# Shared expert: unit 3's gate products ahead of unit 2's up products, and the lower part of the second token half on GpSimd

## The chip, the cores and the metric

One core of one Trainium2 chip. The metric is the device time of one execution in microseconds (us), as the median of several runs. Engines are called by their names in the profile: PE is TensorE (PEld its weight loads), DVE is VectorE, ACT is ScalarE, POOL is GpSimd, SP is SyncE, which only issues DMAs here.

## The reference

A mixture of experts with all eight routed experts taken and one shared expert, with a residual. B = 8 batches of S = 128 tokens, D = 128, F = 512, all float32:

```python
g = jnp.einsum('bsd,edf->ebsf', h, Wg)
u = jnp.einsum('bsd,edf->ebsf', h, Wu)
expert_outs = jnp.einsum('ebsf,efd->ebsd', jax.nn.silu(g) * u, Wd)
expert_output = jnp.einsum('be,ebsd->bsd', gating_probs, expert_outs)
shared = jnp.einsum('bsf,fd->bsd', jax.nn.silu(h @ Sg) * (h @ Su), Sd)
sg = shared_gate_prob[:, :, None]
return x + (1.0 - sg) * expert_output + sg * shared
```

## The kernel before

The 1024 tokens are two halves of 512 columns (`HALVES`), tokens along the free axis and the model width along the partitions. F is cut into four slices of 128. An expert is eight *units*: unit k is slice k % 4 of half k // 4. For a unit TensorE computes the gate product into a PSUM bank `g_ps`, the up product into `u_ps`, and, two units later (`LAG`), adds the unit's share of the down product to `y_ps`. ACT applies silu to `g_ps`; DVE multiplies with `u_ps` into `h_ps` (`hidden`, L408); ACT rounds that to `h_hi` (`hidden_hi`, L334); DVE subtracts to get `h_lo` (`hidden_lo`, L413). In this text gate(k), up(k), down(k), silu(k), hidden(k), h_hi(k) and h_lo(k) are these steps of unit k.

Precision: every float32 operand is split into an upper part in a rounded format (`_hi`) and the remainder (`_lo`), and each product is three matmuls, hi x hi, hi x lo and lo x hi. So each of gate, up and down is three matmuls of 128x512, nine a unit. The upper parts are copies (`first_hi`, `w_hi_slice`, `xs_hi_half`), the lower parts differences (`first_lo`, `slice_lo`, `half_lo` on POOL; `hidden_lo` on DVE).

Each engine runs its own program, written out by hand in order, and engines meet at semaphores: a `wait_ge` holds its engine, and what stands behind it, until the counter is there. There are two banks each of `g_ps`, `u_ps` and `h_ps`: gate(k) waits for silu(k-2), up(k) for hidden(k-2), hidden(k) for h_lo(k-2).

The shared expert comes first, with the weights in buffer 0. Its units 0 and 1 are written out apart (L515 to L540) while tokens and weights still arrive. Units 2 to 7 are the loop at L542: gate(k), up(k), down(k-2). Its first waits also cover the prepared operands:

```python
                pe.wait_ge(first_dve_hi, 2)
                pe.wait_ge(first_pool_lo, 4 if k == BANKS else 5)
```

`first_dve_hi` 2 is DVE's CAST of the shared down weights (`first_hi(DOWN, 0, 4)`, L436, executed at L385); `first_pool_lo` 4 and 5 are the first slice and the other three slices of their lower part on POOL (L234, L235, executed at L224), which wait for that CAST.

The second token half reaches the core as `x_blk`, is turned by DVE (L400) into `x_t[:, 1]`, rounded by ACT (`second_x_hi`, L316, semaphore `x_hi_done[2]`), and DVE takes the difference `x_lo[:, 1]` at L440. gate(4) is the first to use it.

DVE's order in this stage is: hidden(0), CAST of the down weights, hidden(1), h_lo(0), `x_lo` of the second half (L440), hidden(2), h_lo(1), `factors` (L424 and L428, the coefficients of experts and batches), hidden(3), h_lo(2), hidden(4), h_lo(3) and so on. POOL's is: the lower parts of the shared gate and up weights, those of the down weights, slice 0 of expert 0's weights (L244), then the scaled tokens (L239) once the factors are there. ACT's is, per unit: silu(k), one piece of preparation for the next expert (`split_next`: L324 or L320), h_hi(k).

SP's load of expert 1 into buffer 0 (L196) waits for `first_pool_lo` 5.

The eight routed experts follow (`routed_expert`), with the same unit and nine matmuls of 128x512 each; then the end: two output forms, by DVE's transpose and by TensorE.

Of the kernel before, what the change touches and what calls it, by code (L numbers as in the profile page):

```python
# [8 lines left out]
ALU = mybir.AluOpType  # L9
# [4 lines left out]
LAG = 2  # L14
BANKS = 2
# [9 lines left out]
def build(nc, x, gates, shared_gate, Wg, Wu, Wd, Sg, Su, Sd, out):  # L25
# [3 lines left out]
    NF = F // P  # L29
    UNITS = NF * HALVES  # L30
# [18 lines left out]
    with ctx:  # L49
        def sbuf(name, shape, dtype):  # L50
            return ctx.enter_context(nc.sbuf_tensor(name, shape, dtype))

        def sem(name):
            return ctx.enter_context(nc.semaphore(name))
# [5 lines left out]
        x_t = sbuf("x_t", [P, HALVES, N], FP32)  # L60
        x_hi = sbuf("x_hi", [P, HALVES, N], FP32R)
        x_lo = sbuf("x_lo", [P, HALVES, N], FP32R)
# [25 lines left out]
        def banks(name, n):  # L88
            return [ctx.enter_context(nc.psum_tensor(f"{name}{i}", [P, N], FP32)) for i in range(n)]

        y_ps = banks("y_ps", HALVES)
        g_ps = banks("g_ps", BANKS)
        u_ps = banks("u_ps", BANKS)
# [18 lines left out]
        x_hi_done = [sem(f"x_hi_done{i}") for i in range(3)]  # L112
        first_gate_hi = sem("first_gate_hi")
        x_lo_done = sem("x_lo_done")
        x_t_done = sem("x_t_done")
        x1_turned = sem("x1_turned")
        first_act_hi = sem("first_act_hi")
# [2 lines left out]
        first_pool_lo = sem("first_pool_lo")  # L120
# [31 lines left out]
        def f32(t):  # L152
            return t.bitcast(FP32)

        def tokens(t):

            return t.rearrange("p (q b r) -> p q b r", q=NQ, b=HBATCH)

        def by_batch(c):

            return c.unsqueeze(1).unsqueeze(3).to_broadcast([P, NQ, HBATCH, PER])
# [55 lines left out]
        def gpsimd_program(pool):  # L217
            pool.memset(ident[:, :], 0.0).then_inc(ident_zeroed, 1)
            pool.wait_ge(ident_zeroed, 1)
            pool.affine_select(out=ident[:, :], in_=ident[:, :], compare_op=ALU.not_equal, fill=1.0,  # L220
                               base=0, pattern=[[-1, P]], channel_multiplier=1).then_inc(ident_built, 1)

            def first_lo(k, n, m):
                pool.tensor_tensor(w_lo[0][:, k, n:m, :], w_raw[0][:, k, n:m, :],  # L224
                                   f32(w_hi[0][:, k, n:m, :]), ALU.subtract).then_inc(first_pool_lo, 1)

            pool.wait_ge(first_act_hi, 1)
            first_lo(GATE, 2, 4)
            pool.wait_ge(first_act_hi, 2)
            first_lo(UP, 0, 2)  # L230
            pool.wait_ge(first_dve_hi, 1)
            first_lo(UP, 2, 4)
            pool.wait_ge(first_dve_hi, 2)
            first_lo(DOWN, 0, 1)  # L234
            first_lo(DOWN, 1, 4)  # L235

            def scale(e, h):
                c = coef[:, e - 1, h * HBATCH:(h + 1) * HBATCH]
                pool.tensor_tensor(tokens(xs[:, h, :]), tokens(x_t[:, h, :]), by_batch(c), ALU.mult)\  # L239
                    .then_inc(xs_done, 1)  # L240

            def slice_lo(n, buf, slices_before):
                pool.wait_ge(w_hi_done, slices_before + n + 1)
                pool.tensor_tensor(w_lo[buf][:, :, n, :], w_raw[buf][:, :, n, :],  # L244
                                   f32(w_hi[buf][:, :, n, :]), ALU.subtract).then_inc(w_lo_done, 1)

            def half_lo(h, buf, halves_before):
                pool.wait_ge(xs_hi_done, halves_before + h + 1)
                pool.tensor_tensor(xs_lo[buf][:, h, :], xs[:, h, :], f32(xs_hi[buf][:, h, :]),  # L249
                                   ALU.subtract).then_inc(xs_lo_done, 1)  # L250

            def prepare(e, buf, halves_before, slices_before):
                for h in range(HALVES):

                    pool.wait_ge(xs_hi_done, halves_before - HALVES + h + 1)
                    pool.wait_ge(xs_lo_done, halves_before - HALVES + h + 1)
                    scale(e, h)
                for kind, n in PREPARE:
                    if kind == "slice":
                        slice_lo(n, buf, slices_before)  # L260
                    else:
                        half_lo(n, buf, halves_before)


            slice_lo(0, 1, 0)
            pool.wait_ge(coef_ready, 1)
            pool.wait_ge(x_t_done, 2)
            pool.wait_ge(x1_turned, 1)
            for h in range(HALVES):
                scale(1, h)  # L270
            slice_lo(1, 1, 0)
            half_lo(0, 1, 0)
            slice_lo(2, 1, 0)
            half_lo(1, 1, 0)
            slice_lo(3, 1, 0)
            with pool.Fori(0, E // 2 - 1) as i:
                for q in range(2):
                    prepare(2 * i + 2 + q, q, 2 * HALVES * i + HALVES * (q + 1),
                            2 * NF * i + NF * (q + 1))
            prepare(E, 0, HALVES * (E - 1), NF * (E - 1))  # L280

            for h in range(HALVES):
                pool.wait_ge(base_scaled, h + 1)
                pool.tensor_tensor(base_t[:, h, :], base_t[:, h, :], x_t[:, h, :], ALU.add)\
                    .then_inc(base_done, 1)
# [97 lines left out]
        def vector_program(dve):  # L383
# [27 lines left out]
            def hidden_lo(n, k):  # L411
                dve.wait_ge(h_hi_done, n + 1)
                dve.tensor_tensor(h_lo[k % HB][:, :], h_ps[k % BANKS][:, :], f32(h_hi[k % HB][:, :]),  # L413
                                  ALU.subtract).then_inc(h_lo_done, 1)
# [7 lines left out]
            def factors():  # L422
                dve.wait_ge(sg_loaded, DMA)
                dve.tensor_scalar(not_sg[:, :], coef[:, E, :], -1.0, 1.0, ALU.mult, ALU.add)\  # L424
                   .then_inc(one_minus, 1)
                dve.wait_ge(gates_loaded, DMA)
                dve.wait_ge(one_minus, 1)
                dve.tensor_tensor(coef[:, 0:E, :].rearrange("p e b -> p b e"), gates_sb[:, :, :],  # L428
                                  not_sg[:, :].unsqueeze(2).to_broadcast([P, B, E]), ALU.mult)\
                   .then_inc(coef_ready, 1)  # L430
# [5 lines left out]
            first_hi(DOWN, 0, 4)  # L436
            hidden(1, 1, first=True)
            hidden_lo(0, 0)
            dve.wait_ge(x_hi_done[2], 1)
            dve.tensor_tensor(x_lo[:, 1, :], x_t[:, 1, :], f32(x_hi[:, 1, :]), ALU.subtract)\  # L440
               .then_inc(x_lo_done, 1)
            for k in range(2, UNITS):
                hidden(k, k)
                hidden_lo(k - 1, k - 1)
                if k == 2:
                    factors()
            for k in range(UNITS):
                hidden(UNITS + k, k)
                hidden_lo(UNITS + k - 1, (k - 1) % UNITS)
# [30 lines left out]
        def tensor_program(pe):  # L480
# [58 lines left out]
                pe.matmul(u_ps[f][:, :], w_lo[0][:, UP, f, :], x_hi[:, 0, :], start=False, stop=True,  # L539
                          skip_group_check=True).then_inc(up_done, 1)  # L540

            for k in range(BANKS, UNITS):  # L542
                f, h = k % NF, k // NF
                g, u = g_ps[k % BANKS], u_ps[k % BANKS]
                if k == NF:
                    pe.wait_ge(x_hi_done[2], 1)
                    pe.wait_ge(x_lo_done, 3)
                pe.wait_ge(silu_done, k - BANKS + 1)
                pe.wait_ge(first_act_hi, 1)
                pe.matmul(g[:, :], w_hi[0][:, GATE, f, :], x_hi[:, h, :], start=True, stop=False)  # L550
                pe.matmul(g[:, :], w_hi[0][:, GATE, f, :], x_lo[:, h, :], start=False, stop=False)  # L551
                pe.wait_ge(first_pool_lo, 1)
                pe.matmul(g[:, :], w_lo[0][:, GATE, f, :], x_hi[:, h, :], start=False, stop=True)\  # L553
                  .then_inc(gate_done, 1)
                pe.wait_ge(hidden_done, k - BANKS + 1)
                pe.wait_ge(first_dve_hi, 1)
                pe.matmul(u[:, :], w_hi[0][:, UP, f, :], x_hi[:, h, :], start=True, stop=False)  # L557
                pe.matmul(u[:, :], w_hi[0][:, UP, f, :], x_lo[:, h, :], start=False, stop=False)  # L558
                pe.wait_ge(first_pool_lo, 3)
                pe.matmul(u[:, :], w_lo[0][:, UP, f, :], x_hi[:, h, :], start=False, stop=True)\  # L560
                  .then_inc(up_done, 1)
                pe.wait_ge(first_dve_hi, 2)
                pe.wait_ge(first_pool_lo, 4 if k == BANKS else 5)
                if k == LAG:

                    pe.wait_ge(x_t_done, 1)
                down(k - LAG, k - LAG, 0, begin=(k - LAG) % NF == 0)
# [61 lines left out]
        scalar_program(nc.scalar)  # L629
        vector_program(nc.vector)  # L630
        tensor_program(nc.tensor)


# [23 lines left out]
```

## Time and profile before

| | us |
|---|---|
| median of 3 runs | 157.64 (157.46 to 157.65) |
| the profiled execution | 157.71 |
| its span, first to last instruction | 156.4 |
| PE busy | 153.3 (98%) |
| PEld busy | 124.6 (80%) |
| ACT busy | 109.2 (70%) |
| DVE busy | 99.4 (64%) |
| POOL busy | 75.9 (49%) |
| granted TensorE clock, mean | 0.999 |

Between the profiled execution's time and its span lie 1.3 us. Times in the rows count from the span's start. A matmul's record is longer than its share, since matmuls are pipelined: the distance between the starts of two is what one costs. The records of two instructions of DVE, ACT or POOL that follow without a wait overlap a little. A bracket at a row's end is idle time of the engine before the instruction, and what ended it. In a form such as `128x512 fp32r<-128x512 f32`, the left is what is written, the right what is read. `xN` merges N instructions of one line.

### The profile page before, as it was taken

The numbers are of one execution on the slowest core, as the hardware profiler recorded it, in microseconds if no ns is written. First come the engines' busy times: TensorE is split into PE (matmuls) and PEld (weight loads), VectorE is DVE, ScalarE is ACT, GpSimd is POOL, SyncE is SP. The second block draws the span as 40 slices with busy tenths as digits, with TensorE's granted clock in tenths as the row PEclk, the third lists the DMA queues.
The fourth block names the chain that finished last, engine by engine and source line by source line (L and its number), as shares of the span: only waits on it lengthen the run. The fifth ranks groups of instructions, "written<-read, shape, count | busy, mean of one in ns | idle before, by whom it ended". The sixth has DMA issues, their size and how long they took to land.

```text
span 156.4 us, 2310 instructions
## 1 busy us (share of the span) xinstructions
PE 153.3 (98%) x674; PEld 124.6 (80%) x674; DVE 99.4 (64%) x160; ACT 109.2 (70%) x202; POOL 75.9 (49%) x77
## 2 busy tenths in 40 slices
PE   7999999999999999999999999999999999999993
PEld 2868888888888888888888888888888888888873
DVE  0598767766666666666666666656665666666692
ACT  4778867877577757785877667766777677755541
POOL 1448882556455463547255825573547355660000
PEclk9999999999999999999999999999999999999999
DMA  5856006003300240006000500060000000000006
GB/s 151 209 186 201 0 5 196 4 2 101 102 0 0 51 155 0 0 5 196 0 0 0 201 0 0 0 198 3 0 0 2 0 0 0 0 0 4 0 0 134
DMA packets 12727, 8.24 MB, mean 53 GB/s; under 512 B 5041, under 2 KB 10673, under 8 KB 12721
## 3 DMA queue, kind: packets, MB, share of 16 engines
q1 hardware_dynamic: 12144, 7.64, 17.2%
q10 hardware_dynamic: 576, 0.52, 1.0%
q8 instruction: 3, 0.05, 0.1%
q14 instruction: 4, 0.02, 0.0%
HBM read 7.64 MB, written 0.52 MB: 52 GB/s over the span
## 4 chain that ended last, share of the span: by engine, by line
PE 98%; ACT 0%; issue 0%
PE y_ps L494 10%; PE y_ps L499 10%; PE y_ps L496 10%; PE u_ps L586 9%; PE u_ps L584 9%; PE g_ps L581 9%; PE g_ps L579 9%; PE u_ps L585 9%; PE g_ps L580 9%; PE u_ps L482 2%; PE u_ps L557 1%; PE g_ps L551 1%; PE u_ps L558 1%; PE g_ps L550 1%; PE u_ps L560 1%; PE g_ps L553 1%
## 5 line engine op out<-in xcount | busy, mean ns | idle before, releaser
L408 DVE TENSOR_TENSOR h_ps<-silu,u_ps 128x512 f32<-128x512 f32 x71 | 49.4, 696 | 48.3 <-PE u_ps L586 45.5
L334 ACT ACTIVATE h_hi<-h_ps 128x512 fp32r<-128x512 f32 x71 | 42.6, 600 | 39.0 <-DVE h_ps L408 39.0
L244 POOL TENSOR_TENSOR w_lo<-w_raw,w_hi 128x384 fp32r<-128x384 f32 x32 | 32.4, 1014 | 39.9 <-ACT w_hi L324 39.9
L413 DVE TENSOR_TENSOR h_lo<-h_ps,h_hi 128x512 fp32r<-128x512 f32 x71 | 48.5, 683 | 0.0
L329 ACT ACTIVATE silu<-g_ps 128x512 f32<-128x512 f32 x72 | 43.0, 598 | 0.1
L249 POOL TENSOR_TENSOR xs_lo<-xs,xs_hi 128x512 fp32r<-128x512 f32 x16 | 20.6, 1290 | 16.6 <-ACT xs_hi L320 16.6
L499 PE MATMUL y_ps<-h_lo,w_hi 128*128 128x512 f32 x71 | 27.7, 391 | 0.0
L494 PE MATMUL y_ps<-h_hi,w_lo 128*128 128x512 f32 x71 | 27.7, 390 | 0.0
L496 PE MATMUL y_ps<-h_hi,w_hi 128*128 128x512 f32 x71 | 27.6, 389 | 0.0
L579 PE MATMUL g_ps<-x_hi,w_hi 128*128 128x512 f32 x64 | 24.9, 389 | 0.0
L580 PE MATMUL g_ps<-x_lo,w_hi 128*128 128x512 f32 x64 | 24.9, 389 | 0.0
L581 PE MATMUL g_ps<-x_hi,w_lo 128*128 128x512 f32 x64 | 24.9, 389 | 0.0
L584 PE MATMUL u_ps<-xs_hi,w_hi 128*128 128x512 f32 x64 | 24.9, 389 | 0.0
L585 PE MATMUL u_ps<-xs_lo,w_hi 128*128 128x512 f32 x64 | 24.9, 389 | 0.0
L586 PE MATMUL u_ps<-xs_hi,w_lo 128*128 128x512 f32 x64 | 24.9, 389 | 0.0
L324 ACT ACTIVATE w_hi<-w_raw 128x384 fp32r<-128x384 f32 x32 | 16.6, 518 | 0.2 <-DMA w_raw<-in_L_cond_Wd 0.2
L239 POOL TENSOR_TENSOR xs<-x_t,coef 128x512 f32<-128x512 f32 x16 | 16.3, 1043 | 0.5 <-DVE coef L428 0.5
L499 PEld LDWEIGHTS y_ps<-h_lo,w_hi 128*128 128x128 f32 x71 | 13.3, 188 | 3.2 <-DVE h_lo L413 0.3
L494 PEld LDWEIGHTS y_ps<-h_hi,w_lo 128*128 128x128 f32 x71 | 13.3, 188 | 3.0 <-issue 0.4
L496 PEld LDWEIGHTS y_ps<-h_hi,w_hi 128*128 128x128 f32 x71 | 13.3, 188 | 2.8
L580 PEld LDWEIGHTS g_ps<-x_lo,w_hi 128*128 128x128 f32 x64 | 12.0, 188 | 2.5
L581 PEld LDWEIGHTS g_ps<-x_hi,w_lo 128*128 128x128 f32 x64 | 12.0, 188 | 2.5
(80 smaller groups left out, 119.1 us busy)
## 6 DMA issues: line engine op xcount, KB each, us to landing
w_raw<-in_L_cond_Wg SPq DMA_DIRECT2D x8, 256.0 KB, 2.7
w_raw<-in_L_cond_Wu SPq DMA_DIRECT2D x8, 256.0 KB, 3.0
w_raw<-in_L_cond_Wd SPq DMA_DIRECT2D x8, 256.0 KB, 3.6
w_raw<-in_L_cond_Sg ACTq DMA_DIRECT2D x2, 128.0 KB, 3.1
x_nat<-in_x SPq DMA_DIRECT2D x2, 128.0 KB, 2.9
x_blk<-in_x SPq DMA_DIRECT2D x4, 64.0 KB, 2.9
w_raw<-in_L_cond_Sd SPq DMA_DIRECT2D x1, 256.0 KB, 3.3
out<-y_blk SPq DMA_DIRECT2D x4, 64.0 KB, 2.2
```

The lines of the kernel that those rows point to most:

```text
L329: act.activation(silu[k % BANKS][:, :], g_ps[k % BANKS][:, :], ACT.Silu)\
L334: act.activation(h_hi[k % HB][:, :], h_ps[k % BANKS][:, :], ACT.Copy)\
L408: dve.tensor_tensor((to or h_ps[k % BANKS])[:, :], silu[k % BANKS][:, :], u_ps[k % BANKS][:, :], ALU.mult).then_inc(hidden_done, 1)
L413: dve.tensor_tensor(h_lo[k % HB][:, :], h_ps[k % BANKS][:, :], f32(h_hi[k % HB][:, :]), ALU.subtract).then_inc(h_lo_done, 1)
L494: pe.matmul(y_ps[h][:, :], lo, h_hi[k % HB][:, :], start=begin, stop=False, skip_group_check=True)
L496: pe.matmul(y_ps[h][:, :], hi, h_hi[k % HB][:, :], start=False, stop=False, skip_group_check=True)
L499: pe.matmul(y_ps[h][:, :], hi, h_lo[k % HB][:, :], start=False, stop=f == NF - 1, skip_group_check=True)\
L579: pe.matmul(g[:, :], hi, x_hi[:, h, :], start=True, stop=False)
L580: pe.matmul(g[:, :], hi, x_lo[:, h, :], start=False, stop=False)
L581: pe.matmul(g[:, :], lo, x_hi[:, h, :], start=False, stop=True).then_inc(gate_done, 1)
L584: pe.matmul(u[:, :], hi, xs_hi[buf][:, h, :], start=True, stop=False)
L585: pe.matmul(u[:, :], hi, xs_lo[buf][:, h, :], start=False, stop=False)
```

## The change

Two things. On PE, the loop of the shared expert is cut into two functions, `first_gate` and `first_up`, and the gate products of units 2 and 3 both go ahead of up(2); from unit 4 on the order is as before. And the difference `x_lo[:, 1]` moves from DVE to POOL, between the lower parts of the up weights and those of the down weights, with a semaphore of its own, `second_x_lo`. DVE's order behind it is written anew: h_lo(1) goes ahead of hidden(2), and h_lo(2) ahead of hidden(3), behind the factors.

```diff
@@ -112,6 +112,7 @@
         x_hi_done = [sem(f"x_hi_done{i}") for i in range(3)]
         first_gate_hi = sem("first_gate_hi")
         x_lo_done = sem("x_lo_done")
+        second_x_lo = sem("second_x_lo")
         x_t_done = sem("x_t_done")
         x1_turned = sem("x1_turned")
         first_act_hi = sem("first_act_hi")
@@ -230,6 +231,9 @@
             first_lo(UP, 0, 2)
             pool.wait_ge(first_dve_hi, 1)
             first_lo(UP, 2, 4)
+            pool.wait_ge(x_hi_done[2], 1)
+            pool.tensor_tensor(x_lo[:, 1, :], x_t[:, 1, :], f32(x_hi[:, 1, :]), ALU.subtract)\
+                .then_inc(second_x_lo, 1)
             pool.wait_ge(first_dve_hi, 2)
             first_lo(DOWN, 0, 1)
             first_lo(DOWN, 1, 4)
@@ -436,14 +440,14 @@
             first_hi(DOWN, 0, 4)
             hidden(1, 1, first=True)
             hidden_lo(0, 0)
-            dve.wait_ge(x_hi_done[2], 1)
-            dve.tensor_tensor(x_lo[:, 1, :], x_t[:, 1, :], f32(x_hi[:, 1, :]), ALU.subtract)\
-               .then_inc(x_lo_done, 1)
-            for k in range(2, UNITS):
+            hidden_lo(1, 1)
+            hidden(2, 2)
+            factors()
+            hidden_lo(2, 2)
+            hidden(3, 3)
+            for k in range(4, UNITS):
                 hidden(k, k)
                 hidden_lo(k - 1, k - 1)
-                if k == 2:
-                    factors()
             for k in range(UNITS):
                 hidden(UNITS + k, k)
                 hidden_lo(UNITS + k - 1, (k - 1) % UNITS)
@@ -539,12 +543,12 @@
                 pe.matmul(u_ps[f][:, :], w_lo[0][:, UP, f, :], x_hi[:, 0, :], start=False, stop=True,
                           skip_group_check=True).then_inc(up_done, 1)
 
-            for k in range(BANKS, UNITS):
+            def first_gate(k):
                 f, h = k % NF, k // NF
-                g, u = g_ps[k % BANKS], u_ps[k % BANKS]
+                g = g_ps[k % BANKS]
                 if k == NF:
                     pe.wait_ge(x_hi_done[2], 1)
-                    pe.wait_ge(x_lo_done, 3)
+                    pe.wait_ge(second_x_lo, 1)
                 pe.wait_ge(silu_done, k - BANKS + 1)
                 pe.wait_ge(first_act_hi, 1)
                 pe.matmul(g[:, :], w_hi[0][:, GATE, f, :], x_hi[:, h, :], start=True, stop=False)
@@ -552,6 +556,10 @@
                 pe.wait_ge(first_pool_lo, 1)
                 pe.matmul(g[:, :], w_lo[0][:, GATE, f, :], x_hi[:, h, :], start=False, stop=True)\
                   .then_inc(gate_done, 1)
+
+            def first_up(k):
+                f, h = k % NF, k // NF
+                u = u_ps[k % BANKS]
                 pe.wait_ge(hidden_done, k - BANKS + 1)
                 pe.wait_ge(first_dve_hi, 1)
                 pe.matmul(u[:, :], w_hi[0][:, UP, f, :], x_hi[:, h, :], start=True, stop=False)
@@ -559,8 +567,16 @@
                 pe.wait_ge(first_pool_lo, 3)
                 pe.matmul(u[:, :], w_lo[0][:, UP, f, :], x_hi[:, h, :], start=False, stop=True)\
                   .then_inc(up_done, 1)
+
+
+            first_gate(LAG)
+            first_gate(LAG + 1)
+            for k in range(LAG, UNITS):
+                if k > LAG + 1:
+                    first_gate(k)
+                first_up(k)
                 pe.wait_ge(first_dve_hi, 2)
-                pe.wait_ge(first_pool_lo, 4 if k == BANKS else 5)
+                pe.wait_ge(first_pool_lo, 4 if k == LAG else 5)
                 if k == LAG:
 
                     pe.wait_ge(x_t_done, 1)
```

On PE, from the shared expert's unit 2 on, before (the digit at a tile's name is its buffer; `w_hi0` holds the shared expert's weights):

```order
L550 MATMUL g_ps0<-x_hi,w_hi0 128x512 [waits first_act_hi,silu_done]
L551 MATMUL g_ps0<-x_lo,w_hi0 128x512
L553 MATMUL g_ps0<-x_hi,w_lo0 128x512 [waits first_pool_lo]
L557 MATMUL u_ps0<-x_hi,w_hi0 128x512 [waits first_dve_hi,hidden_done]
L558 MATMUL u_ps0<-x_lo,w_hi0 128x512
L560 MATMUL u_ps0<-x_hi,w_lo0 128x512 [waits first_pool_lo]
L494 MATMUL y_ps0<-h_hi0,w_lo0 128x512 [waits x_t_done,h_hi_done,first_pool_lo,first_dve_hi]
L496 MATMUL y_ps0<-h_hi0,w_hi0 128x512
L499 MATMUL y_ps0<-h_lo0,w_hi0 128x512 [waits h_lo_done]
L550 MATMUL g_ps1<-x_hi,w_hi0 128x512 [waits first_act_hi,silu_done]
```

and now:

```order
L557 MATMUL g_ps0<-x_hi,w_lo0 128x512 [waits first_pool_lo]
L554 MATMUL g_ps1<-x_hi,w_hi0 128x512 [waits first_act_hi,silu_done]
L555 MATMUL g_ps1<-x_lo,w_hi0 128x512
L557 MATMUL g_ps1<-x_hi,w_lo0 128x512 [waits first_pool_lo]
L565 MATMUL u_ps0<-x_hi,w_hi0 128x512 [waits first_dve_hi,hidden_done]
L566 MATMUL u_ps0<-x_lo,w_hi0 128x512
L568 MATMUL u_ps0<-x_hi,w_lo0 128x512 [waits first_pool_lo]
L498 MATMUL y_ps0<-h_hi0,w_lo0 128x512 [waits x_t_done,h_hi_done,first_pool_lo,first_dve_hi]
L500 MATMUL y_ps0<-h_hi0,w_hi0 128x512
L503 MATMUL y_ps0<-h_lo0,w_hi0 128x512 [waits h_lo_done]
L565 MATMUL u_ps1<-x_hi,w_hi0 128x512 [waits first_dve_hi,hidden_done]
```

The three products into `g_ps1` stood behind down(0) and stand ahead of up(2).

On DVE, from the CAST of the down weights on, before:

```order
L385 CAST w_hi0<-w_raw0 128x512 [waits first_down_loaded]
L408 TENSOR_TENSOR h_ps1<-silu1,u_ps1 128x512 [waits up_done,silu_done]
L413 TENSOR_TENSOR h_lo0<-h_ps0,h_hi0 128x512 [waits h_hi_done]
L440 TENSOR_TENSOR x_lo<-x_t,x_hi 128x512 [waits x_hi_done2]
L408 TENSOR_TENSOR h_ps0<-silu0,u_ps0 128x512 [waits h_lo_done,up_done,silu_done]
L413 TENSOR_TENSOR h_lo1<-h_ps1,h_hi1 128x512 [waits h_hi_done]
L424 TENSOR_SCALAR not_sg<-coef 128x8 [waits sg_loaded]
L428 TENSOR_TENSOR coef<-gates_sb,not_sg 128x8x8 [waits one_minus,gates_loaded]
L408 TENSOR_TENSOR h_ps1<-silu1,u_ps1 128x512 [waits h_lo_done,up_done,silu_done]
L413 TENSOR_TENSOR h_lo2<-h_ps0,h_hi2 128x512 [waits h_hi_done]
```

and now:

```order
L389 CAST w_hi0<-w_raw0 128x512 [waits first_down_loaded]
L412 TENSOR_TENSOR h_ps1<-silu1,u_ps1 128x512 [waits up_done,silu_done]
L417 TENSOR_TENSOR h_lo0<-h_ps0,h_hi0 128x512 [waits h_hi_done]
L417 TENSOR_TENSOR h_lo1<-h_ps1,h_hi1 128x512 [waits h_hi_done]
L412 TENSOR_TENSOR h_ps0<-silu0,u_ps0 128x512 [waits h_lo_done,up_done,silu_done]
L428 TENSOR_SCALAR not_sg<-coef 128x8 [waits sg_loaded]
L432 TENSOR_TENSOR coef<-gates_sb,not_sg 128x8x8 [waits one_minus,gates_loaded]
L417 TENSOR_TENSOR h_lo2<-h_ps0,h_hi2 128x512 [waits h_hi_done]
L412 TENSOR_TENSOR h_ps1<-silu1,u_ps1 128x512 [waits h_lo_done,up_done,silu_done]
```

`x_lo` is gone from here, and h_lo(1) and h_lo(2) each stand ahead of the next unit's product.

On POOL, behind the lower parts of the gate and up weights, now:

```order
L225 TENSOR_TENSOR w_lo0<-w_raw0,w_hi0 128x256 [waits first_dve_hi]
L235 TENSOR_TENSOR x_lo<-x_t,x_hi 128x512 [waits x_hi_done2]
L225 TENSOR_TENSOR w_lo0<-w_raw0,w_hi0 128x128 [waits first_dve_hi]
L225 TENSOR_TENSOR w_lo0<-w_raw0,w_hi0 128x384
L248 TENSOR_TENSOR w_lo1<-w_raw1,w_hi1 128x3x128 [waits w_hi_done]
```

Only the row of L235 is new; the others stood in this order before.

## Rows read from the trace of the kernel before

**Rows 1.** The chain of work that ended last, by engine, share of the span

```profile
PE 98%; ACT 0%; issue 0%
```

**Rows 2.** Timeline of TensorE, units 2 to 6: start us, us, instruction, [idle before]

```profile
8.27 0.39 PE L550 MATMUL g_ps<-x_hi,w_hi 128*128 128x512 f32 x1
...
9.09 0.50 PE L557 MATMUL u_ps<-x_hi,w_hi 128*128 128x512 f32 x1
...
10.01 0.47 PE L494 MATMUL y_ps<-h_hi,w_lo 128*128 128x512 f32 x1
10.31 0.40 PE L496 MATMUL y_ps<-h_hi,w_hi 128*128 128x512 f32 x1
10.62 0.50 PE L499 MATMUL y_ps<-h_lo,w_hi 128*128 128x512 f32 x1
10.95 0.39 PE L550 MATMUL g_ps<-x_hi,w_hi 128*128 128x512 f32 x1
...
17.13 0.39 PE L550 MATMUL g_ps<-x_hi,w_hi 128*128 128x512 f32 x1
```

**Rows 3.** Timeline of DVE, 5.9 to 18.2 us

```profile
5.99 0.28 DVE L385 CAST w_hi<-w_raw 128x256 fp32r<-128x256 f32 x1
...
8.35 0.70 DVE L408 TENSOR_TENSOR h_ps<-silu,u_ps 128x512 f32<-128x512 f32 x1 [0.29 <-PE u_ps L539]
8.95 0.42 DVE L385 CAST w_hi<-w_raw 128x512 fp32r<-128x512 f32 x1
9.28 0.69 DVE L408 TENSOR_TENSOR h_ps<-silu,u_ps 128x512 f32<-128x512 f32 x1
9.88 0.68 DVE L413 TENSOR_TENSOR h_lo<-h_ps,h_hi 128x512 fp32r<-128x512 f32 x1
10.48 0.94 DVE L440 TENSOR_TENSOR x_lo<-x_t,x_hi 128x512 fp32r<-128x512 f32 x1
11.35 0.68 DVE L408 TENSOR_TENSOR h_ps<-silu,u_ps 128x512 f32<-128x512 f32 x1
...
12.54 0.36 DVE L424 TENSOR_SCALAR not_sg<-coef 128x8 f32<-128x8 f32 x1
13.01 0.28 DVE L428 TENSOR_TENSOR coef<-gates_sb,not_sg 128x64 f32<-128x64 f32 x1
13.18 0.70 DVE L408 TENSOR_TENSOR h_ps<-silu,u_ps 128x512 f32<-128x512 f32 x1
...
15.64 0.68 DVE L413 TENSOR_TENSOR h_lo<-h_ps,h_hi 128x512 fp32r<-128x512 f32 x1
...
17.49 0.68 DVE L413 TENSOR_TENSOR h_lo<-h_ps,h_hi 128x512 fp32r<-128x512 f32 x1
```

**Rows 4.** Timeline of ACT, 8 to 12 us, and the first split of expert 1

```profile
8.08 0.63 ACT L316 ACTIVATE x_hi<-x_t 128x512 fp32r<-128x512 f32 x1
...
10.50 0.59 ACT L329 ACTIVATE silu<-g_ps 128x512 f32<-128x512 f32 x1
11.25 0.53 ACT L324 ACTIVATE w_hi<-w_raw 128x384 fp32r<-128x384 f32 x1 [0.15 <-DMA w_raw<-in_L_cond_Wd]
...
26.67 0.52 ACT L324 ACTIVATE w_hi<-w_raw 128x384 fp32r<-128x384 f32 x1
```

**Rows 5.** Timeline of POOL, 6 to 18 us

```profile
6.00 0.86 POOL L224 TENSOR_TENSOR w_lo<-w_raw,w_hi 128x256 fp32r<-128x256 f32 x1 [4.52 <-ACT w_hi L296]
...
7.53 0.73 POOL L224 TENSOR_TENSOR w_lo<-w_raw,w_hi 128x256 fp32r<-128x256 f32 x1
9.45 0.46 POOL L224 TENSOR_TENSOR w_lo<-w_raw,w_hi 128x128 fp32r<-128x128 f32 x1 [1.19 <-DVE w_hi L385]
9.87 1.01 POOL L224 TENSOR_TENSOR w_lo<-w_raw,w_hi 128x384 fp32r<-128x384 f32 x1
11.85 1.02 POOL L244 TENSOR_TENSOR w_lo<-w_raw,w_hi 128x384 fp32r<-128x384 f32 x1 [0.98 <-ACT w_hi L324]
...
16.34 1.29 POOL L249 TENSOR_TENSOR xs_lo<-xs,xs_hi 128x512 fp32r<-128x512 f32 x1
```

## The prediction

> **What bounds the kernel now.** I read the chain that ended last first. It is TensorE's from one end to the other [rows 1], so a change can only pay by removing a pause of TensorE, and costs whatever pause it adds. Next TensorE's timeline [rows 2]: from 10.95 us (unit 3's first gate product) to 17.13 (unit 6's) lie 27 products in 6.18 us, 0.229 each, 2.06 per unit, with no pause. Unit 2 alone takes longer: from 8.27 to 10.95 are 2.68 us, 0.62 over that pace. It pauses three times: at 9.09 for hidden(0), which ends at 8.35 + 0.70 = 9.05 on DVE [rows 3]; at 10.01 for the first slice of the down weights' lower part, which ends at 9.45 + 0.46 = 9.91 on POOL [rows 5]; at 10.62 for h_lo(0), which ends at 9.88 + 0.68 = 10.56 [rows 3]. So TensorE follows a DVE end by 0.05 and a POOL end by 0.10, and the product behind a pause comes 0.30 to 0.33 after it and not 0.23: a pause costs 0.1 more than the wait. The same way ACT and DVE follow each other by 0.03 and POOL follows by 0.08, and an instruction that waits for nothing starts 0.09 (DVE), 0.11 (ACT) or 0.04 (POOL) before the end of the one before it.
>
> **Gate products of unit 3 first.** Three products fill the first pause. up(2) starts at 8.27 + 6 x 0.228 = 9.64, when hidden(0) is long done; down(0) is due at 10.32, its h_lo product at 10.78 (h_lo(0) is there at 10.56), and up(3) at 11.01, where it stood at 10.95 + 0.69 = 11.64 before. Taken alone this is worth 0.63 us. Nothing is added: TensorE runs the same products.
>
> **The lower part on POOL.** It waits for ACT's x_hi of the second half, which ends at 8.08 + 0.63 = 8.71 [rows 4], so it starts at 8.79. Its price is that of the same form on POOL, 1.29 us (L249) [rows 5]; it ends at 10.09. Both pieces of the down weights stand behind it on that queue. On DVE 0.94 us go away at 10.48 [rows 3], but hidden(2), next there, waits for ACT's silu(2), 10.50 + 0.59 = 11.09 [rows 4], and so gains under 0.1.
>
> **What POOL's instruction does to DVE.** Rows of before show pairs that overlapped:
> - DVE's L440 (128x512, both inputs in SBUF) started at 10.48 while POOL worked from 9.87 to 10.88. It took 0.94, where products of this size take 0.68, and ended 0.54 after POOL [rows 3, 5].
> - DVE's L424 has 8 elements and took 0.36, more than the 0.28 of L428 with 64; it ended at 12.90, POOL's L244 at 12.87.
> - DVE's CAST at 5.99 and POOL's L224 at 6.00: here POOL paid, 0.86 where the same form takes 0.73. The CAST was 0.01 ahead.
> - L413 at 9.88, with one input in PSUM, ran beside POOL in its usual 0.68.
>
> So CASTs, the L424 form and SBUF-only differences keep POOL out or are kept out, and who starts first wins. In the new order POOL's difference starts at 8.79 and DVE's CAST of the down weights at 8.95, 0.16 later. I let the CAST wait for POOL's end. L440 ended 0.54 after POOL, 0.14 less than its own 0.68; so the CAST (0.42) ends 0.28 after 10.09, at 10.37 instead of 9.37: **1.00 us late**.
>
> By L440 alone the second one could also be slowed rather than stopped: it lost 0.26 of 0.40 shared. Slowed at that rate, the CAST does 0.40 of its 0.42 by 10.09, ends near 10.1, and all behind it comes 0.27 earlier: a sum of +0.69. I take the stop, because L424, with 8 elements, did not get through beside POOL either and ended just as POOL did.
>
> The Trainium skill, SBUF — State Buffer, section "Who interferes with whom", speaks against this change: a DVE copy or cast in a two-port mode, or a DVE instruction with two SBUF inputs against a GpSimd instruction that reads SBUF, takes an exclusive lock for the whole instruction, and whoever issues second blocks fully. By that rule the sum is the forecast's and not +0.69.
>
> **From the CAST to TensorE.** hidden(1) starts at 10.28 (9.28 before), h_lo(0) at 10.88 and ends at 11.56. POOL's down slice waits for the CAST too: 10.45 to 10.91; the rest 10.87 to 11.88. TensorE: down(0) was due at 10.32 and starts at 10.91 + 0.10 = 11.01, the next at 11.31, the h_lo product at 11.56 + 0.05 = 11.61, up(3) at 11.94. Before it was 11.64. **First term: +0.30**; the whole 0.63 is gone. SP's load of expert 1 goes out 1.0 later too, and is first used at 26.67 [rows 4], far off.
>
> **Second term, the factors.** h_hi(1), and with it silu(2) behind it on ACT, come 1.00 later: silu(2) 11.50 to 12.10, hidden(2) at 12.24, the factors at 12.84. ACT's w_hi slice (0.53) is at 11.98 to 12.51, POOL's L244 starts at 12.59 and ends at 13.60, and L424 is stuck behind it to 13.65. L428 then runs 13.75 to 14.04. The new order puts h_lo(2) ahead of hidden(3): 13.95, then 14.55 for hidden(3), against 13.18 before. From hidden(3)'s start to h_lo(3)'s end the trace has 15.64 + 0.68 - 13.18 = 3.14 (ACT's h_hi, silu(4) and its split lie between) [rows 3]; that gives 17.69. TensorE wants it for the last product ahead of unit 6's, due at 17.13 - 0.23 + 0.30 = 17.20. It waits to 17.74, and unit 6 starts at 18.07 and not 17.13: **+0.94 to +0.96 in all**, where the first +0.30 is contained. Then DVE gains on TensorE: its h_lo rows stand 1.85 apart (15.64, 17.49) [rows 3] against 2.06, so no third pause comes, and nothing later gives time back, as TensorE never pauses after.
>
> **Sum.** 157.71 of the profiled execution (156.4 span, 1.3 around it) + 0.96 = 158.67. The median of the runs is 0.07 lower, 157.64, so I forecast **158.6**. Ends: with L424 not stuck in its new place the chain is 0.34 shorter, +0.62; if POOL's difference pays 0.13 more, as the 0.86 row did, +1.09. The forecast's own range is thus 158.2 to 158.8.
>
> **Rivals.**
> 1. *The CAST wins the race.* 0.16 us between two starts is small; one hangs on a DMA (the transpose before L316), the other on TensorE. Then the CAST keeps 9.37 and POOL ends near 10.52 (its work starts some 0.14 after its record, by the 0.86 row). The down slice ends at 10.94, down(0) starts at 11.04, up(3) at 11.80: +0.16. L424 is stuck to 12.92 as before, hidden(3) is at 13.82, h_lo(3) at 16.96, just in time. 157.8. Against it: the row at 5.99 shows 0.01 us to be enough.
> 2. *CAST and POOL don't hinder each other, L424 and POOL do.* down(0) waits only for POOL's slice, 10.04 to 10.50: starts at 10.60, up(3) 11.38, -0.26. But hidden(3) at 13.82, h_lo(3) at 16.96, needed at 16.64; unit 6 at 17.34: +0.21. 157.85. Against it: the 0.86 row.
> 3. *Nothing hinders anything*, the rival that is not slower: -0.26 stays, 157.4. It decides if the CAST's record stays at 0.42 and L424's falls to some 0.2. The reordering is sound, and the waits of rows 2 are real; against it stand L440 and L424, which had no other reason to be long.
>
> **How the numbers follow.** This kernel's measurement can tell 0.2%, 0.32 us, from no change. Forecast: 0.66. Rival 1: 0.10, rival 2: 0.07, both within 0.2%. Rival 3: 0.14, of which 0.09 within 0.2% and 0.05 beyond it (if POOL's slice is not late either, up to -0.63). Something longer still: 0.03, slower. Faster 0.05, same 0.26, slower 0.69. The range reaches from rival 1 and 2 to the forecast's upper end with 0.1 to spare: 157.7 to 158.9; rival 3 and half of the rest lie outside.
>
> **What would show it.** Right: a CAST of the down weights of about 1.4 us from 8.95 that ends 0.3 after POOL's x_lo; hidden(1) near 10.3; TensorE's down(0) near 11.0; L424's counterpart about 0.8 long; h_lo(3)'s product 0.5 late; unit 6 near 18.1. Wrong: a CAST of 0.42, or one that starts before POOL's record, or TensorE's up(3) before 11.6.

## The result and the profile after

The changed kernel takes 158.19 us (157.75 to 158.65, 12 runs) against 157.53 us (157.32 to 158.01, 12 runs) before: a ratio of 1.0037, interval 1.0025 to 1.0049, so slower by 0.4 to 0.8 us. The forecast was slower, 158.6 in a range of 157.7 to 158.9. The measured median lies in that range, just under the forecast's own 158.2 to 158.8.

The profiled execution (157.92) is not the forecast's case: its CAST took 0.42 and started ahead of POOL's x_lo, two of the signs that the prediction named for being wrong. DVE's and ACT's lines stand four further down in the changed kernel: L424 of before is L428, and L428 is L432. The execution's timelines, in the order of TensorE, ACT, DVE and POOL (start us, us, instruction, idle before):

```profile
8.38 0.39 PE L554 MATMUL g_ps<-x_hi,w_hi 128*128 128x512 f32 x1
...
11.15 0.47 PE L498 MATMUL y_ps<-h_hi,w_lo 128*128 128x512 f32 x1 [0.56 <-issue]
...
11.93 0.40 PE L565 MATMUL u_ps<-x_hi,w_hi 128*128 128x512 f32 x1
...
21.45 0.39 PE L595 MATMUL g_ps<-x_hi,w_hi 128*128 128x512 f32 x1
...
8.50 0.63 ACT L320 ACTIVATE x_hi<-x_t 128x512 fp32r<-128x512 f32 x1 [0.45 <-DVE x_t L404]
...
7.76 0.71 DVE L404 STREAM_TRANSPOSE x_t<-x_blk 128x512 f32<-128x512 f32 x1 [1.45 <-DMA x_blk<-in_x]
...
9.06 0.42 DVE L389 CAST w_hi<-w_raw 128x512 fp32r<-128x512 f32 x1
...
12.22 0.92 DVE L432 TENSOR_TENSOR coef<-gates_sb,not_sg 128x64 f32<-128x64 f32 x1
...
13.61 0.68 DVE L412 TENSOR_TENSOR h_ps<-silu,u_ps 128x512 f32<-128x512 f32 x1
...
9.21 1.42 POOL L235 TENSOR_TENSOR x_lo<-x_t,x_hi 128x512 fp32r<-128x512 f32 x1 [0.91 <-ACT x_hi L320]
...
11.98 1.02 POOL L248 TENSOR_TENSOR w_lo<-w_raw,w_hi 128x384 fp32r<-128x384 f32 x1
```

The same transpose in the kernel before:

```profile
7.34 0.71 DVE L400 STREAM_TRANSPOSE x_t<-x_blk 128x512 f32<-128x512 f32 x1 [1.06 <-DMA x_blk<-in_x]
```

ACT's x_hi ends at 9.13 and not at 8.71 as in [rows 4], since DVE's transpose waited 0.4 longer for the DMA of the second token half. So the CAST started 0.15 ahead of POOL's x_lo, kept its 0.42, and POOL paid 0.13 (1.42 for 1.29). That is rival 1, with one difference: of the factors L428 got through, and L432, with 64 elements, was held up (0.92 for 0.28, to 0.14 after the end of POOL's L248). down(0) still starts at 11.15 and not 10.43 (up(2) at 9.75, three products), behind the down slice on POOL.

I compare executions by the **stretch** from unit 2's first gate product to unit 8's. From unit 8's start to the end of the device time it is 136.47 to 136.50 us in each of the 14 profiles of this study, while unit 2's start moves from 7.48 to 8.38 between them. Before, the stretch went from 8.27 [rows 2] to 21.21, 12.94; here it is 13.07: +0.13. A stretch can be set beside 12.94 only where no landing holds DVE or ACT back inside it; in e5, e6 and e7 below, where unit 2 starts earliest, one does.

### The profile page after: what moved, and what is told of

It reads as the page before. It is cut to its first block, busy times and chain, and to the rows that moved or that the text cites. A ratio compares the mean times of both kernels' runs of the same rounds, so it can differ in the third digit from the quotient of the medians.

```text
span 156.6 us, 2310 instructions
## 1 busy us (share of the span) xinstructions
PE 152.9 (98%) x674; PEld 124.9 (80%) x674; DVE 99.0 (63%) x159; ACT 108.9 (70%) x202; POOL 77.4 (49%) x78
## 4 chain that ended last, share of the span: by engine, by line
PE 98%; issue 0%; ACT 0%
PE y_ps L498 10%; PE y_ps L500 10%; PE y_ps L503 10%; PE u_ps L601 9%; PE u_ps L600 9%; PE g_ps L596 9%; PE g_ps L595 9%; PE u_ps L602 9%; PE g_ps L597 9%; PE u_ps L486 2%; PE u_ps L565 1%; PE u_ps L566 1%; PE g_ps L554 1%; PE g_ps L555 1%; PE g_ps L557 1%; PE u_ps L568 1%
## 5 line engine op out<-in xcount | busy, mean ns | idle before, releaser
L248 POOL TENSOR_TENSOR w_lo<-w_raw,w_hi 128x384 fp32r<-128x384 f32 x32 | 32.6, 1018 | 38.9 <-ACT w_hi L328 38.9
L595 PEld LDWEIGHTS g_ps<-x_hi,w_hi 128*128 128x128 f32 x64 | 12.0, 188 | 2.5
```

Of the source, the lines that this page charges most:

```text
L595: pe.matmul(g[:, :], hi, x_hi[:, h, :], start=True, stop=False)
```

## Experiments

### The two kernels profiled again

**look_change_1**, **look_change_2**: the changed kernel, unaltered. The first expectation counts the profiles of e1 to e4, which stand below.

> The changed kernel, unaltered, looked at once more. In four of the five profiles that exist by now the second token half was rounded well ahead of the CAST (x_hi ends 0.3 to 0.5 before the CAST's place, 0.24 before it in the profile of before, and 0.08 after it in the one of the change). Theory A: where x_hi is ready so early, POOL's x_lo starts first, the CAST takes about 1.1 us and ends 0.28 after POOL, down(0) waits about 0.4 to 0.7, and from unit 2's first gate product to unit 8's lie 13.6 to 13.9 us (12.94 in the profile of before, 13.07 in that of the change). Theory B: the CAST stays at 0.42 and that stretch at 13.1, whichever started first.

> The changed kernel once more. Theory A: CAST of 1.3 to 1.5 and a stretch of 13.7 to 13.95 if POOL's x_lo starts first, CAST of 0.42 and a stretch of 13.05 to 13.3 if not; nothing in between. The first is the likelier, as in look_change_1.

They took 158.16 and 158.56. look_change_1's timelines of DVE, POOL and TensorE:

```profile
8.45 1.50 DVE L389 CAST w_hi<-w_raw 128x512 fp32r<-128x512 f32 x1
...
12.42 0.78 DVE L428 TENSOR_SCALAR not_sg<-coef 128x8 f32<-128x8 f32 x1
...
14.05 0.68 DVE L412 TENSOR_TENSOR h_ps<-silu,u_ps 128x512 f32<-128x512 f32 x1
...
8.37 1.30 POOL L235 TENSOR_TENSOR x_lo<-x_t,x_hi 128x512 fp32r<-128x512 f32 x1 [0.66 <-ACT x_hi L320]
...
12.16 1.02 POOL L248 TENSOR_TENSOR w_lo<-w_raw,w_hi 128x384 fp32r<-128x384 f32 x1 [0.71 <-ACT w_hi L328]
...
7.77 0.39 PE L554 MATMUL g_ps<-x_hi,w_hi 128*128 128x512 f32 x1
...
10.59 0.47 PE L498 MATMUL y_ps<-h_hi,w_lo 128*128 128x512 f32 x1 [0.61 <-DVE w_hi L389]
...
11.54 0.39 PE L565 MATMUL u_ps<-x_hi,w_hi 128*128 128x512 f32 x1
...
17.23 0.50 PE L503 MATMUL y_ps<-h_lo,w_hi 128*128 128x512 f32 x1 [0.30 <-DVE h_lo L417]
17.57 0.39 PE L554 MATMUL g_ps<-x_hi,w_hi 128*128 128x512 f32 x1
...
21.69 0.39 PE L595 MATMUL g_ps<-x_hi,w_hi 128*128 128x512 f32 x1
```

This is the forecast, row by row. POOL started 0.08 ahead; the CAST ends at 9.95, 0.28 after POOL's 9.67; L428's 8 elements end at 13.20, 0.02 after POOL's 13.18; TensorE pauses for down(0) and again at h_lo(3). Unit 6 starts 9.80 after unit 2, as forecast (18.07 - 8.27). The stretch is 13.92: +0.98. DVE and POOL of look_change_2, and then three pieces of its chain of work (start us, us, what):

```profile
8.39 0.70 DVE L412 TENSOR_TENSOR h_ps<-silu,u_ps 128x512 f32<-128x512 f32 x1 [0.36 <-PE u_ps L543]
9.16 1.19 DVE L389 CAST w_hi<-w_raw 128x512 fp32r<-128x512 f32 x1
...
8.77 1.30 POOL L235 TENSOR_TENSOR x_lo<-x_t,x_hi 128x512 fp32r<-128x512 f32 x1 [0.71 <-ACT x_hi L320]
```

```profile
4.95 4.19 DMA w_raw<-in_L_cond_Sd
9.14 0.02 issue
9.16 0.04 DVE w_hi L389
```

POOL started 0.39 ahead, the CAST took 1.19 and ended 0.28 after POOL, and the stretch is 13.76: +0.82. The CAST also started late here: 0.77 after hidden(0)'s start, where it is 0.60 in [rows 3], because the shared down weights (`in_L_cond_Sd`) landed only at 9.14. So both starts can hang on a DMA, and not x_lo's alone. The 0.17 cost nothing in this execution, since POOL held the CAST longer than that.

**look_before_1**, **look_before_2**: the kernel before, unaltered.

> The kernel before, unaltered, looked at again. The stretch from unit 2's first gate product to unit 8's was 12.95 us in its first profile, where that product started at 8.27. In the experiments it starts anywhere from 7.48 to 8.38, with the landing of the first tokens. If the pauses of unit 2 are bound to TensorE's own start, the stretch stays at 12.9 to 13.0; if some of what TensorE waits for is bound to a later landing, the stretch is longer where the start is earlier (13.1 to 13.3 for a start near 7.7).

> The same again: a third point of how the stretch of the kernel before goes with its start, and the differences L424 and L440 behind POOL: theory A expects both to end right after the POOL instruction that overlaps them (L440 0.55 after, L424 0.03 after) and to have their plain durations, 0.68 and 0.16, where none does.

157.50 and 157.52. The starts were 8.04 and 8.07, the stretches 12.97 and 12.96: over these 0.23 us the stretch does not depend on the start. L440 took 0.94 in both and ended 0.55 after POOL, as expected. L424 and the POOL instruction it meets, look_before_1 and then look_before_2:

```profile
12.33 0.18 DVE L424 TENSOR_SCALAR not_sg<-coef 128x8 f32<-128x8 f32 x1
...
11.47 1.02 POOL L244 TENSOR_TENSOR w_lo<-w_raw,w_hi 128x384 fp32r<-128x384 f32 x1 [0.81 <-ACT w_hi L324]
```

```profile
12.34 0.60 DVE L424 TENSOR_SCALAR not_sg<-coef 128x8 f32<-128x8 f32 x1
...
11.90 1.01 POOL L244 TENSOR_TENSOR w_lo<-w_raw,w_hi 128x384 fp32r<-128x384 f32 x1 [1.23 <-ACT w_hi L324]
```

With POOL nearly done (12.49) L424 takes 0.18; with POOL busy to 12.91 it takes 0.60. Same instruction, same data, same start: only POOL's place differs.

### Who starts first, forced both ways

**e1_cast_first**:

```diff
+            pool.wait_ge(first_dve_hi, 2)
             pool.wait_ge(x_hi_done[2], 1)
             pool.tensor_tensor(x_lo[:, 1, :], x_t[:, 1, :], f32(x_hi[:, 1, :]), ALU.subtract)\
                 .then_inc(second_x_lo, 1)
-            pool.wait_ge(first_dve_hi, 2)
             first_lo(DOWN, 0, 1)
```

> The changed kernel, but POOL's x_lo waits for DVE's CAST of the down weights, so the CAST always wins. Theory A (the two exclude each other, and who starts first is decided by when the DMA of the second token half lands): the CAST keeps 0.42, POOL's x_lo starts 0.08 behind it, near 9.45, the first down slice ends near 11.2, TensorE's down(0) starts near 11.3; all executions alike, +0.4 us against before (0.2 more than where the CAST wins by itself, as x_lo starts later), with a spread like that of before. Theory B (no exclusion; x_lo only delays what is queued behind it on POOL): x_lo now starts 0.66 later than it can, so this is slower than the change: +1.2 or more. Theory C (the cost is in the new place of the factors alone): same as the changed kernel, +0.65.

157.82 against 157.61, ratio 1.0014 (1.0003 to 1.0025): +0.2, 0.2 less than expected, though its profile's stretch, 13.34, is +0.40. Making POOL wait longer made the kernel faster than the change (the two intervals meet at 1.0025). That refutes B, and C as the whole cause, as the factors stood where the change has them. One thing that theory A expected did not come: with the order fixed, the executions should have spread no wider than those of before, and they lie from 157.36 to 158.27, as far apart as those of the change.

**e2_cast_waits**:

```diff
             dve.wait_ge(first_down_loaded, DMA)
+            dve.wait_ge(second_x_lo, 1)
             first_hi(DOWN, 0, 4)
```

> The changed kernel, but DVE's CAST waits until POOL's x_lo is done, so the stop of the forecast happens in every execution. Theory A: like the slow executions of the change or some 0.2 slower (the CAST starts after POOL instead of in its last part), +1.15 us against before where the second token half lands early, up to +1.5 where it lands 0.4 later. Theory B: the changed kernel never had such a stop, so all its executions lie at least 0.4 below this one's fastest. Theory C: +1.0 or more as well.

```profile
9.66 0.43 DVE L389 CAST w_hi<-w_raw 128x512 fp32r<-128x512 f32 x1 [1.09 <-POOL x_lo L235]
```

158.38 against 157.61, ratio 1.0055 (1.0040 to 1.0071): +0.77, where +1.15 was expected; the stretch of the profile, 14.01, is +1.07. That execution (158.27) began unit 2 at 7.79, 0.25 to 0.48 ahead of the three profiles of before; whether the others did too is not known. A stop put there on purpose looks like look_change_1: a CAST that ends at 10.09, and pauses at down(0) and h_lo(3). By theory B all executions of the change would lie at least 0.4 under this kernel's fastest, 158.27; they reach 158.65.

### x_lo behind the down slices

**e3_down_first**; **e4_factors_late** adds the second piece:

```diff
-            pool.wait_ge(x_hi_done[2], 1)
-            pool.tensor_tensor(x_lo[:, 1, :], x_t[:, 1, :], f32(x_hi[:, 1, :]), ALU.subtract)\
-                .then_inc(second_x_lo, 1)
             pool.wait_ge(first_dve_hi, 2)
             first_lo(DOWN, 0, 1)
             first_lo(DOWN, 1, 4)
+            pool.wait_ge(x_hi_done[2], 1)
+            pool.tensor_tensor(x_lo[:, 1, :], x_t[:, 1, :], f32(x_hi[:, 1, :]), ALU.subtract)\
+                .then_inc(second_x_lo, 1)
...
-            factors()
             hidden_lo(2, 2)
             hidden(3, 3)
+            factors()
```

> The changed kernel, but on POOL x_lo stands behind both pieces of the down weights' lower part. The CAST meets no POOL instruction. Theory A: the first pause of TensorE is gone (down(0) at 10.3, up(3) at 11.0), the factors are still stuck behind POOL, hidden(3) is near 13.8, and TensorE waits for h_lo(3) instead; +0.2 us against before in every execution. Theory B: here too the queue behind x_lo is freed: -0.25 or better. Theory C: like the change, +0.65, as the factors stand where they stood.

> As e3_down_first, and the factors on DVE go behind hidden(3), so their wait for POOL holds up neither h_lo(2) nor hidden(3). Theory A: hidden(3) near 13.2, TensorE waits only some 0.2 for h_lo(3); -0.37 us against before. Theory B: the factors were never stuck, so this is like e3_down_first within 0.1. Theory C: the whole cost goes away, -0.4 or better.

e3: 157.61 against 157.61, ratio 1.0000 (0.9990 to 1.0011); stretch 13.09, +0.15. The median lies midway between what theory A (+0.2) and theory B (-0.25) expected; the rows below decide for A. e4: 157.32, ratio 0.9982 (0.9970 to 0.9994), -0.3, where -0.37 was expected; stretch 12.59, -0.35. The two intervals overlap a little. TensorE and DVE of e3:

```profile
8.05 0.39 PE L554 MATMUL g_ps<-x_hi,w_hi 128*128 128x512 f32 x1
...
12.16 0.39 PE L554 MATMUL g_ps<-x_hi,w_hi 128*128 128x512 f32 x1
...
16.70 0.50 PE L503 MATMUL y_ps<-h_lo,w_hi 128*128 128x512 f32 x1 [0.53 <-DVE h_lo L417]
17.04 0.40 PE L554 MATMUL g_ps<-x_hi,w_hi 128*128 128x512 f32 x1
...
8.74 0.42 DVE L389 CAST w_hi<-w_raw 128x512 fp32r<-128x512 f32 x1
...
12.06 1.01 DVE L432 TENSOR_TENSOR coef<-gates_sb,not_sg 128x64 f32<-128x64 f32 x1
```

and of e4:

```profile
8.14 0.39 PE L554 MATMUL g_ps<-x_hi,w_hi 128*128 128x512 f32 x1
...
12.27 0.40 PE L554 MATMUL g_ps<-x_hi,w_hi 128*128 128x512 f32 x1
...
16.26 0.50 PE L503 MATMUL y_ps<-h_lo,w_hi 128*128 128x512 f32 x1
16.59 0.39 PE L554 MATMUL g_ps<-x_hi,w_hi 128*128 128x512 f32 x1
...
12.47 0.69 DVE L417 TENSOR_TENSOR h_lo<-h_ps,h_hi 128x512 fp32r<-128x512 f32 x1 [0.67 <-ACT h_hi L338]
...
13.94 0.28 DVE L432 TENSOR_TENSOR coef<-gates_sb,not_sg 128x64 f32<-128x64 f32 x1
```

and of the kernel before, gate(4):

```profile
13.03 0.40 PE L550 MATMUL g_ps<-x_hi,w_hi 128*128 128x512 f32 x1
```

From gate(2) to gate(4) it is 4.11 in e3 and 4.13 in e4, where it was 13.03 - 8.27 = 4.76: up to there the clean gain of 0.63 is whole. In e3 the first pause is gone, the factors are stuck (1.01 for 0.28), and the whole gain goes into one pause at h_lo(3). In e4 the factors meet no POOL instruction and that pause shrinks from 0.7 to 0.1. It was their wait and not their work that cost: DVE sits idle for 0.67 ahead of h_lo(2) in e4, room enough for 0.16 + 0.28. So the forecast's two causes can be taken away one by one, and each gives time back: the stop of the CAST and the late down slice (e3 against the change, both at once), and the factors' wait (e4 against e3).

**e8_factors_only**: the second piece of that diff alone, on the changed kernel.

> The changed kernel with one edit: the factors on DVE go behind hidden(3). x_lo stays ahead of the down slices, so the CAST is still stopped. Theory A (two terms): the first, the late down slice and h_lo(0), stays, and part of the second goes: hidden(3) no longer waits for POOL, but silu(2) is late by the stop: +0.4 against before (+0.3 to +0.6), 0.25 better than the change. Theory C (factors alone): 0.0 or better. Theory B: as the change.

```profile
8.98 1.17 DVE L389 CAST w_hi<-w_raw 128x512 fp32r<-128x512 f32 x1
...
8.58 1.29 POOL L235 TENSOR_TENSOR x_lo<-x_t,x_hi 128x512 fp32r<-128x512 f32 x1 [0.37 <-ACT x_hi L320]
```

157.95 against 157.63, ratio 1.0019 (1.0002 to 1.0036): +0.3, the lower end of what was expected. The profile has POOL's x_lo first by 0.40, a CAST of 1.17 that ends 0.28 after it, and a stretch of 13.39, +0.45. look_change_2, with the same lead of POOL (0.39), had 13.76: the factors' wait is worth 0.37 beside the stop too.

### One half of the change at a time

**e5_gates_only**: TensorE's new order with the DVE and POOL programs of before. **e6_pool_only**: the kernel before, with the three lines of x_lo taken from DVE and put on POOL ahead of the down slices, as in the change.

> Of the change only TensorE's new order; x_lo and everything else on DVE and POOL as before. The first pause is filled, but h_lo(1) still stands behind x_lo and hidden(2) on DVE and ends near 12.6, where down(1)'s last product is now due near 12.15: by theory A the whole gain of 0.6 goes into that wait, 0.0 against before (within 0.1). A rival that holds the first pause alone to count expects -0.4 to -0.6.

> Of the change only the move of x_lo to POOL; TensorE's and DVE's orders as before (L440 left out of DVE's). Theory A: the stop of the CAST by itself costs all that the change costs: +0.75 to +0.95 us against before. Theory B: +0.3 at most, for the down slice behind x_lo on POOL. Theory C (the factors' new place costs): 0.0, as they keep their place.

e5: 157.56 against 157.52, ratio 1.0007 (0.9995 to 1.0020): nothing, as expected. e6: 158.41 against 157.52, ratio 1.0055 (1.0040 to 1.0071): +0.9. Of e5, TensorE and DVE:

```profile
7.48 0.39 PE L550 MATMUL g_ps<-x_hi,w_hi 128*128 128x512 f32 x1
...
12.13 0.50 PE L499 MATMUL y_ps<-h_lo,w_hi 128*128 128x512 f32 x1 [0.41 <-DVE h_lo L413]
...
7.55 0.70 DVE L408 TENSOR_TENSOR h_ps<-silu,u_ps 128x512 f32<-128x512 f32 x1
8.39 0.43 DVE L385 CAST w_hi<-w_raw 128x512 fp32r<-128x512 f32 x1
...
11.40 0.68 DVE L413 TENSOR_TENSOR h_lo<-h_ps,h_hi 128x512 fp32r<-128x512 f32 x1
```

h_lo(1), behind x_lo and hidden(2) on DVE, is what TensorE waits for instead. This execution (157.35) shows why its stretch, 13.38, can't be set beside 12.94: unit 2 began 0.8 earlier than in [rows 2], but the down weights landed at 8.36 (that chain has `4.94 3.42 DMA w_raw<-in_L_cond_Sd`), so the CAST stands 0.84 and not 0.60 behind hidden(0)'s start, and all behind it on DVE is late against TensorE. Of e6, TensorE, DVE and POOL:

```profile
10.51 0.47 PE L495 MATMUL y_ps<-h_hi,w_lo 128*128 128x512 f32 x1 [0.95 <-POOL w_lo L225]
...
8.44 0.41 DVE L389 CAST w_hi<-w_raw 128x512 fp32r<-128x512 f32 x1
...
8.69 1.31 POOL L235 TENSOR_TENSOR x_lo<-x_t,x_hi 128x512 fp32r<-128x512 f32 x1 [1.05 <-ACT x_hi L320]
```

The number came as theory A expected, but this profile not by its mechanism: the CAST was first and not stopped. TensorE's down(0) waits for POOL's down slice, which stands behind x_lo, and pauses for it (0.95 in the row). So the queue on POOL is a cost of its own. How large is open. The profiled execution (157.97) is the fastest of the six, +0.45 over before's median, which is already more than theory B's +0.3; its stretch, 13.84, is +0.90, but unit 2 began at 7.66, 0.4 to 0.6 ahead of the three profiles of before, and x_lo hung on a landing that came only 0.1 earlier (DVE's transpose starts at 7.23, and in the kernel before at 7.34). Whether the slower five had the stop is not known. With TensorE's new order and the CAST first too, the profile of the change had only +0.13.

### A version that beats both

**e7_silu_early**, on top of e4:

```diff
             hidden_hi(0, 0)
+            silu_of(2, 2)
             hidden_hi(1, 1)
             for k in range(BANKS, UNITS):
-                silu_of(k, k)
+                if k > 2:
+                    silu_of(k, k)
...
-            hidden_lo(1, 1)
             hidden(2, 2)
+            hidden_lo(1, 1)
```

> As e4_factors_late, and ACT takes silu(2) ahead of h_hi(1), and DVE hidden(2) ahead of h_lo(1). Theory A: hidden(2) starts near 10.6 and not 11.2 (counted with unit 2's first gate product at 8.27), h_lo(3) is there in time, no pause of TensorE is left from unit 2 on: -0.65 us against before. If e4's last pause comes from something else than the chain from silu(2) to h_lo(3), this is no faster than e4, -0.3.

157.05 against 157.52, ratio 0.9971 (0.9960 to 0.9982): -0.3 to -0.6, about 0.2 better than e4 (the two intervals overlap) and 0.2 short of the expected. ACT's row shows the likely reason:

```profile
11.20 0.53 ACT L328 ACTIVATE w_hi<-w_raw 128x384 fp32r<-128x384 f32 x1 [0.94 <-DMA w_raw<-in_L_cond_Wd]
```

hidden(2) starts at 10.29, but ACT then waits 0.94 for expert 0's weights ahead of h_hi(2). TensorE started unit 2 at 7.74 here, ahead of every profile of before, so h_lo(3) was still 0.2 late. That the landing is the reason in the other executions too was not tested.

## Why the prediction was right, and where it was off

- **The clean gain, 0.63.** Right in size up to gate(4), 0.65 and 0.63 in e3 and e4. But it cannot be had by itself: e5 loses it to h_lo(1), and with both causes of loss taken away e4 and e7 still keep only 0.3 and 0.5. The prediction did not say that the next chain on DVE was due so soon.
- **POOL's price and place.** 1.29 forecast, 1.30 found (look_change_1).
- **The stop of the CAST.** Forecast to end 0.28 after POOL, found 0.28 after it three times, whether the two had shared 1.22 us (look_change_1), 0.91 (look_change_2) or 0.89 (e8). An instruction that is slowed would end later the shorter it had shared: at L440's rate about when POOL did in the first, and 0.1 after it in the other two. So it is stopped, not slowed. L424 at 0.18 and at 0.60 shows the same in the kernel before.
- **First and second term.** In the stopped case +0.94 to +0.96 forecast, +0.98 and +0.82 found, with both pauses in their places. The first alone, at up(3), was forecast at +0.30 and found at +0.39 and +0.25.
- **The step that was off** is in the rivals: "0.16 us between two starts" was given one outcome with 0.66 and the other with 0.10. Both happen, from one execution to the next. Of three profiles of the change two have the stop and one, the first seen, has not: 158.56 and 158.16 against 157.92. Rival 1's +0.16 was +0.13. So 158.6 describes one case, and the median, 0.66 over before, lies between the cases. That it fell just under the forecast's own range, and well inside the wide one, is in part luck: it depends on how often each order comes.
- The prediction had one start hang on a DMA and the other on TensorE. In look_change_2 the CAST's hung on a DMA too.
- The stop is also shorter the later the CAST starts behind POOL: 1.08 longer than 0.42 with POOL 0.08 ahead, 0.77 with 0.39. The prediction took one distance, that of a single profile.

What share of the executions has the stop is open: only the profiled ones show it. The spread of the change (157.75 to 158.65) is wider than before's, but is no evidence for two cases: e1, where only one order is possible, spreads as widely (157.36 to 158.27). Where that spread comes from is open.

## What to carry to other kernels

Before a difference or copy moves from DVE to GpSimd, look which DVE instructions will run beside it: here a cast and operations with all inputs in SBUF, started behind it, were held up until it ended, and what they cost is what stands behind them. Started 0.15 ahead of it, the cast kept its time and GpSimd paid 0.13. Look also at what stands behind the moved instruction on GpSimd's queue, and at the next chain that is due when a pause is filled. Where two starts are a tenth of a microsecond apart and one hangs on a DMA, plan for both orders, or fix the order with a wait as e1 did: +0.2 and not +0.66.

## What was not expected of the hardware

Landings move enough between executions of one program to change who is first: x_hi ended 0.07 after the CAST's start (after), 0.16 before it (look_change_1) and 0.47 before it (look_change_2); of the last, 0.17 is the CAST's own wait for the down weights. And an 8-element DVE instruction can take 0.16 (e8), 0.36, 0.60 or 0.78 us, by what is left of the GpSimd instruction that it meets.
